# A round of two steps with three blocks of pairs, four single banks for the maxima, and twelve steps ahead

## The chip, the core and the metric

One core of a Trainium2 chip. The metric is device time in microseconds (us), the median of several executions; durations come from one execution under the hardware profiler. TensorE (PE) multiplies, VectorE (DVE) and ScalarE (ACT) read its results out of PSUM (eight banks of 512 float32 columns on 128 partitions), GpSimd (POOL) works in SBUF, SyncE (SP) and GpSimd issue transfers.

## What is computed

Input x is [4, 1024, 128]. Two layers, each with a residual:

```python
x = x + attn(layernorm(x))      # time mixing with a decaying scan (k, v, r), per batch
x = x + ffn(layernorm(x))       # below
# ffn: six nodes, each a multi-head attention over 1024 tokens, 8 heads of 16 columns
for c in range(6):
    nsrc = min(c + 1, 5); snode = c - nsrc
    q = ew[c, 0] * (nodes[c - 1] @ We[eq] + be[eq])
    k = ew[c, 1] * (nodes[snode] @ We[ek] + be[ek])
    v = ew[c, 2] * (nodes[snode + nsrc // 2] @ We[ev] + be[ev])
    nodes[c] = act_w[c] * mha(q, k, v, Wq[c], Wk[c], Wv[c], Wo[c]) + q
out = layernorm(nodes[5])
```

The softmax needs the maximum of each query's scores over all keys, since the scores are large here.

## The kernel before

**Units, groups, steps.** One attention (a node c of a batch b) is a unit; there are 24, in the order BATCH_OF. A unit has 4 groups (4 heads of one half of the queries: HG = 4, NHALF = 2), a group has 8 steps (NCH = 8 chunks of 128 keys). So a unit has UC = 32 steps and the whole has STEPS = 768. One step makes four score tiles (`scores`, L526: a chunk's 128 keys by 512 queries of one head, in one of three PSUM banks "ring"), ScalarE turns each into exponentials (L853, into `e_ring` with ten slots), and the value product (`weighted`, L571, L588: four heads side by side in the array, 512 query columns, float32) adds them up in the context bank over the group's eight steps.

**Maxima.** LOOKAHEAD = 14 steps ahead of the scores of a group, its scores are multiplied a first time the other way round (`maxima` of TensorE, L545, L566: 128 queries by 512 keys, two products a tile for the 1024 keys) into one of two double banks (`wide`, `WIDE_BANKS`), and VectorE reduces the 1024 columns to one maximum (`maxima` of VectorE, L1127, L1133). A group has 16 tiles, two to a step. When a group is finished (`finished`, L292, at s + LOOKAHEAD = 0 modulo 8), VectorE splits the maxima in two parts and transposes them (`split_high`, `split_low`, `turn_squares`: L1138, L1142, L1151), SP stores the rows and loads them one step later into two extra rows of `q_aug` (`store_rows`, `load_rows`: L1403, L1415), so that the second score product subtracts the maximum by itself.

**TensorE's order** is written out by hand (L660 to L695). A step is two halves. In each half: score, maxima, score, maxima, where a score and the maxima product behind it use different rows of the array and start together (a pair); then a half (256 columns) of the value product of the step before. In a step that has an extra product (`product_of`: the k, q and v products of the next units, the output products of the one before, final transposes; `KH_AT`, `OUT_AT`, `TURN_AT`, `V_AT`, `QH_AT`), that product stands in place of the first half's value product, in a ring bank, and the value product is done whole in the second half. A maxima tile waits until VectorE has reduced the tile two before (`v_mx`, L555).

**Before step 0** there is a stage of LOOKAHEAD steps with maxima only, with fillers (L426) and the time mixing of the first batches between (`mix`, at the places of MIX_AT); the mixing of the last parts (i = 6, 7) is spread over units 1 to 5. From ALONE = STEPS - LOOKAHEAD on there are no maxima any more, scores go round five banks. The last group has a way of its own at the end (`project_last`, `last_group`, `last_norm`).

**Other engines.** ScalarE evicts the extra products between the second and third exponential of a step (`stages`, L791) and the context after each group (L868). VectorE evicts v (`evict_v`, L998) and takes the reciprocal of the denominators at step 3 of a unit, second half (L1074). POOL splits k and q in two parts (L1233, L1235) and moves them (L312). SP stores and spreads the reciprocals at step 4 (`spread_rden`, L1443, L1450).

Of the kernel before, what the change touches and what calls it, by code (L numbers as in the profile page):

```python
# [18 lines left out]
LOOKAHEAD = 14  # L19
E_SLOTS = 10  # L20
Q_SLOTS = (0, 1, 0)
# [12 lines left out]
def build(nc, x, time_decay, mix_k, mix_v, mix_r, Wk, Wv, Wr, Wo, ln_g, ln_b, ew, act_w, We, be,  # L34
# [25 lines left out]
    with ctx:  # L60
# [46 lines left out]
        max_neg = sb("max_neg", [P, 2, NR])  # L107
# [28 lines left out]
        wide = [ctx.enter_context(nc.psum_tensor(f"wide{i}", [P, S], F32)) for i in range(2)]  # L136
        context = ctx.enter_context(nc.psum_tensor("context", [P, BANK], F32))
        bank = ([t[:, :] for t in ring] + [t[:, k * BANK:(k + 1) * BANK] for t in wide for k in range(2)] + [context[:, :]])
        WIDE_BANKS, CTX_BANK = ((3, 4), (5, 6)), 7
# [86 lines left out]
        KH_AT, OUT_AT, TURN_AT, V_AT, QH_AT = (5, 9), (13, 17), (18, 19), (21, 25), (30, UC + 1)  # L226
# [7 lines left out]
        FOLDS_AT, VALUES0_AT, ONES_AT = (-13, -12, -10, -8, -7), (-4, -3), 4  # L234
        BIAS0_AT, BIASES_AT = (29, -13), (0, 2)
# [5 lines left out]
        def turns_then_steps(turns, steps=()):  # L241
# [5 lines left out]
            turns_then_steps((7, 7, 8, 17, 17, 17, 17, 17, 18, 21, 24, 24, 28, 29, 30, 30, 31, 31, 32), (-14, -13, -12, -12, -9)),  # L247
            turns_then_steps((7, 8, 21, 23, 26, 26, 26, 26, 28, 29, 29, 29, 32),
# [15 lines left out]
        def final_steps(u):  # L264

            if u + 1 < LAST:
                return (19, 22), (20, 23), (21, 24), 26, 30
            return (19, 21), (20, 22), (21, 23), 24, 28
# [4 lines left out]
        def q_steps(u):  # L273

            if u in (1, 2):
                first = UC * (u - 1)
                return (first + 2, first + 3), first + 5
            first = UC * (u - 2)
            return (first + QH_AT[0], first + QH_AT[1]), first + UC + 3
# [21 lines left out]
        where = {}  # L301

# [42 lines left out]
        def tensor_program(e):  # L345
# [9 lines left out]
            def next_bank():  # L355
                ring_turn[0] += 1
                if alone[0]:
                    return ALONE_BANKS[ring_turn[0] % len(ALONE_BANKS)]
                return (ring_turn[0] - 1) % 3

# [138 lines left out]
            def project_last(at):  # L499

                c, b = CELLS[LAST]
                where["out", LAST, 1] = at
                bk = free_bank(at)
                e.matmul(bk[:, :], w_edge_q[:, c, :], node_ring[:, b, c % 2, half_of(1)], start=True, stop=False)
                e.wait_ge(v_ctx, 1)
                e.matmul(bk[:, :], w_o[0:HG * DH, c, :], ctxT[0:HG * DH, half_of(1)], start=False, stop=False)
                e.wait_ge(a_cv, GROUPS)
                e.wait_ge(g_to_values, 1)
                e.wait_ge(v_mx, GROUPS * TILES)
                e.matmul(bank[WIDE_BANKS[0][0]][:, :], to_values[:, :], last_raw, start=True, stop=True).then_inc(p_last_den, 1)  # L510
                for _ in range(LAST_FILLERS):
                    e.matmul(bank[WIDE_BANKS[1][0]][:, :], w_time_t[:, 0, :], w_time_t[:, 0:CPB, :], start=True, stop=True)
                e.wait_ge(d_w_last, DMA * HG)
                e.wait_ge(v_ctx, 3)
                e.matmul(bk[:, :], w_last[:, :], last_raw, start=False, stop=True).then_inc(p_o, 1)
                freed[at] = (a_oa, 2 * LAST + 2)

            def final_turn(u, hf, at):
                c, b = CELLS[u]
                where["turn", u, hf] = at  # L520
                e.wait_ge(a_oa, 2 * u + 2 if u < LAST else 2 * u + 1 + hf)
                node = node_ring[:, b, (c + 1) % 2, half_of(hf)]
                turn_four(at, halves_of(node), p_ft)
                freed[at] = (a_ft, 2 * b + hf + 1)

# [19 lines left out]
            def maxima(w, kh):  # L545
# [4 lines left out]
                h = hg * HG + hj  # L550
                first = (h % 2) * ROWS
                q0 = qh * BANK + qt * P
                if kh == 0:
                    if w >= 2:
                        e.wait_ge(v_mx, w - 1)  # L555
                    else:
                        for i in WIDE_BANKS[w]:
                            free_bank(i)
# [3 lines left out]
                if u == 0 and qh == 0 and t % (2 * CPB) == 0 and kh == 0:  # L562
                    pair = h // 2
                    e.wait_ge(d_q0[pair], DMA * Q_MOVES)
                    e.wait_ge(d_k0[pair], DMA * K_MOVES)
                done = e.matmul(wide[w % 2][:, half_of(kh)], q_aug[first:first + SPLIT, u % 2, h // 2, q0:q0 + P].bitcast(F32R),  # L566
                                k_aug[first:first + SPLIT, u % 2, h // 2, half_of(kh)].bitcast(F32R), start=True, stop=True)
                if kh == 1:
                    done.then_inc(p_mx, 1)
# [24 lines left out]
            def product_of(s):  # L594

                u, r = divmod(s, UC)
                nxt, prev = u + 1, u - 1
                if 1 <= nxt < UNITS:
                    if r in KH_AT:
                        return lambda: head_k(nxt, KH_AT.index(r), next_bank())  # L600
                    if r in V_AT:
                        return lambda: project_v(nxt, V_AT.index(r), next_bank())
                for unit in (nxt, nxt + 1):
                    if 1 <= unit < UNITS and s in q_steps(unit)[0]:
                        return lambda: head_q(unit, q_steps(unit)[0].index(s), next_bank())
                if 0 <= prev < LAST:
                    if r in OUT_AT:
                        return lambda: project_out(prev, OUT_AT.index(r), next_bank())
                    if CELLS[prev][0] == NODES - 1 and r in TURN_AT:
                        return lambda: final_turn(prev, TURN_AT.index(r), next_bank())  # L610
                for hf, (project_at, turn_at) in enumerate(LAST_AT):
                    if s == project_at:
                        return (lambda: project_last(next_bank())) if hf else (lambda: project_out(LAST, 0, next_bank()))
                    if s == turn_at:
                        return lambda: final_turn(LAST, hf, next_bank())
                return None


# [40 lines left out]

            for s in range(-LOOKAHEAD, LAST_STEP):  # L660
                product = product_of(s)
                z = s - 1
                if s == ALONE:
                    alone[0] = True
                    for w in range(2):
                        freed[WIDE_BANKS[w][1]] = (v_mx, GROUPS * TILES - 1 + w)
                if ALONE <= s < STEPS:
                    for k in range(HG):
                        scores(s, k)
                    if product:  # L670
                        product()
                    weighted(z, slice(0, BANK), True, True)
                    continue
                for half in range(2):
                    w = 2 * (s + LOOKAHEAD) + half
                    for k in range(2):
                        if 0 <= s < STEPS:
                            scores(s, 2 * half + k)
                        if w < GROUPS * TILES:
                            maxima(w, k)  # L680
                    if s < 0:
                        keep_busy(CTX_BANK, BANK // 2)
# [965 lines left out]
```

## Time and profile before

| | us |
|---|---|
| runs of the kernel before | 2264.27, 2265.6 (median), 2288.34 |
| the profiled execution, its own time | 2265.8 |
| its span, first to last instruction | 2264.0 |
| mean granted TensorE clock | 0.998 of full speed |

A busy time is the sum of an engine's instructions; for TensorE their ends are modelled, so what counts there is the distance from start to start. A row of the timeline merges instructions of one kind ("x4") from the start of the first to the end of the last.

### The profile page before, as it was taken

To read this page: it belongs to the slowest core of one execution; us is meant where nothing else is said; L and a number is where in the kernel's file an instruction comes from. 1 tells how busy PE (TensorE), PEld (TensorE's weight loads), DVE (VectorE), ACT (ScalarE), POOL (GpSimd) and SP (SyncE) were. 2 spreads that over 40 slices of the span, in tenths; PEclk is the share of its full clock that TensorE was granted. 3 is DMA by queue.
4 is the path that set the end of the run, shared out by engine and by line. 5 is a ranking of instruction groups with operands and counts; after the bars stand their busy time and mean duration, and the time that the engine had idled before them with its cause. 6 is when DMAs were issued, how large, how long until landed. Compare 5 with 4: busy or idle time off the path is not lost.

```text
span 2264.0 us, 46280 instructions
## 1 busy us (share of the span) xinstructions
PE 2231.4 (99%) x17991; PEld 848.7 (37%) x17991; DVE 2055.1 (91%) x2254; ACT 1829.0 (81%) x3431; POOL 529.3 (23%) x667
## 2 busy tenths in 40 slices
PE   7999999999999999999999999999999999999997
PEld 3533333333333333333333333333333333333332
DVE  6989999999999999999998999999999999989995
ACT  4277888888888888888888888888888888888886
POOL 4431230221312202202112112122022022321313
PEclk9999999999999999999999999999999999999999
DMA  4230332422313314224223233133132242241301
GB/s 126 64 72 25 81 71 49 89 64 66 80 46 91 71 33 92 60 61 85 64 57 81 55 69 80 36 78 80 34 82 62 49 85 54 61 95 42 74 25 53
DMA packets 87546, 149.55 MB, mean 66 GB/s; under 512 B 35147, under 2 KB 49951, under 8 KB 87327
## 3 DMA queue, kind: packets, MB, share of 16 engines
q0 software_dynamic: 28224, 94.13, 19.2%
q1 hardware_dynamic: 59102, 52.46, 9.2%
q8 instruction: 142, 2.33, 0.4%
q14 instruction: 78, 0.63, 0.1%
HBM read 42.36 MB, written 14.91 MB: 25 GB/s over the span
## 4 chain that ended last, share of the span: by engine, by line
PE 95%; DVE 2%; issue 1%; ACT 1%; SPq 0%; POOL 0%; DMA 0%; POOLq 0%; ACTq 0%; DVEq 0%
PE ring L540 43%; PE context L588 36%; PE ring L482 2%; PE ring L471 2%; PE ring L463 2%; PE ring L491 2%; PE ring L496 2%; PE wide L566 2%; DVE max_neg L1133 1%; PE context L426 1%; PE ring L369 0%; ACT e_ring L853 0%; PE ring L394 0%; PE ring L391 0%; PE ring L405 0%
## 5 line engine op out<-in xcount | busy, mean ns | idle before, releaser
L1133 DVE TENSOR_REDUCE max_neg<-wide 128x1 f32<-128x1024 f32 x1536 | 1850.4, 1220 | 142.2 <-PE wide L566 136.4
L853 ACT ACTIVATE e_ring<-ring 128x512 f32<-128x512 f32 x3052 | 1658.2, 597 | 286.6 <-PE ring L540 147.6
L566 PE MATMUL wide<-k_aug,q_aug 48*128 48x512 f32 x3072 | 1121.3, 444 | 2.3 <-DVE max_neg L1133 1.4
L540 PE MATMUL ring<-q_aug,k_aug 50*128 50x512 f32 x3052 | 1114.1, 444 | 0.0
L588 PE MATMUL context<-e_ring,v_aug 128*32 128x256 f32 (+1 forms) x10664 | 938.4, 424 | 1.8 <-ACT raw L868 1.6
L540 PEld LDWEIGHTS ring<-q_aug,k_aug 50*128 50x128 f32 x3052 | 455.7, 184 | 749.7 <-ACT e_ring L853 550.3
L566 PEld LDWEIGHTS wide<-k_aug,q_aug 48*128 48x128 f32 x3072 | 457.9, 184 | 12.9 <-issue 6.5
L588 PEld LDWEIGHTS context<-e_ring,v_aug 128*32 128x32 f32 x10664 | 209.9, 107 | 477.0 <-issue 340.9
L342 POOL DMA_DIRECT2D src<-node_dram x40 | 22.9, 572 | 633.2 <-PE ring L482 633.2
L1233 POOL CAST q_part<-q_part 128x512 fp32r<-128x512 f32 x46 | 28.1, 611 | 476.7 <-ACT q_part L778 302.0
L312 POOL DMA_DIRECT2D q_aug<-q_part x138 | 72.1, 522 | 126.3 <-PE ring L540 126.3
L1190 POOL TENSOR_TENSOR rstd<-vareps,neg_half 128x4 f32<-128x4 f32 x24 | 26.9, 1122 | 219.6 <-DVE vareps L897 219.4
L1259 POOL TENSOR_TENSOR ctxT<-ctxT,rden_bc 128x1024 f32<-128x1024 f32 x23 | 54.7, 2377 | 92.3 <-DMA rden_bc<-rden_dram 92.3
L312 POOL DMA_DIRECT2D k_aug<-k_part x138 | 70.0, 514 | 15.1 <-PE ring L540 9.8
L745 ACT ACTIVATE node_ring<-ring,col 128x512 f32<-128x512 f32 x47 | 32.3, 688 | 48.7 <-PE ring L496 40.8
L1235 POOL TENSOR_TENSOR k_part<-k_part 128x512 f32<-128x512 f32 x47 | 60.3, 1283 | 4.9 <-DVE src L902 1.2
L1235 POOL TENSOR_TENSOR q_part<-q_part 128x512 f32<-128x512 f32 x47 | 60.2, 1281 | 4.0 <-POOL k_part L1235 0.2
L868 ACT ACTIVATE raw<-context 128x512 f32<-128x512 f32 x96 | 58.0, 604 | 0.8 <-PE context L588 0.8
L471 PE MATMUL ring<-node_ring,w_q 128*128 128x512 f32 x92 | 51.8, 645 | 0.1
L491 PE MATMUL ring<-node_ring,w_edge_q 128*128 128x512 f32 x92 | 51.8, 644 | 0.0
L1233 POOL CAST k_part<-k_part 128x512 fp32r<-128x512 f32 x46 | 28.3, 615 | 82.9 <-ACT k_part L764 47.5
L496 PE MATMUL ring<-ctxT,w_o 128*128 128x512 f32 x92 | 47.0, 592 | 0.0
(241 smaller groups left out, 890.8 us busy)
## 6 DMA issues: line engine op xcount, KB each, us to landing
q_aug<-q_part POOLq DMA_DIRECT2D x138, 256.0 KB, 4.5
k_aug<-k_part POOLq DMA_DIRECT2D x138, 256.0 KB, 7.1
src<-node_dram POOLq DMA_DIRECT2D x40, 512.0 KB, 7.2
ctxT<-raw SPq DMA_DIRECT2D x380, 32.0 KB, 2.0
rden_bc<-rden_dram SPq DMA_DIRECT2D x23, 512.0 KB
node_dram<-node_ring SPq DMA_DIRECT2D x16, 512.0 KB, 2.9
q_aug<-rows_dram SPq DMA_DIRECT2D x192, 8.0 KB
node_ring<-in_L_attn_x SPq DMA_DIRECT2D x4, 512.0 KB, 4.9
```

The costliest lines, as they stand in the source:

```text
L312: e.dma_start(aug[first + slot:first + SPLIT:len(slots), u % 2, :, :], part[parity:P:2, slots[slot], :]).then_inc(signal, DMA)
L471: e.matmul(bk[:, :], w_q[:, c, :], node_ring[:, b, c % 2, half_of(hf)], start=True, stop=True).then_inc(p_qh, 1)
L491: e.matmul(bk[:, :], w_edge_q[:, c, :], node_ring[:, b, c % 2, half_of(hf)], start=True, stop=False)
L496: e.matmul(bk[:, :], w_o[:, c, :], ctxT[:, half_of(hf)], start=False, stop=True).then_inc(p_o, 1)
L540: e.matmul(bk[:, :], k_aug[first:first + AUG, u % 2, h // 2, chunk * P:(chunk + 1) * P].bitcast(F32R), q_aug[first:first + AUG, u % 2, h / ...
L566: done = e.matmul(wide[w % 2][:, half_of(kh)], q_aug[first:first + SPLIT, u % 2, h // 2, q0:q0 + P].bitcast(F32R), k_aug[first:first + SPL ...
L588: done = e.matmul(bank[CTX_BANK][j * VW:(j + 1) * VW, columns], v_aug[:, u % 2, chunk, hg * HG + j, :], e_ring[:, (HG * z + order_of(z).in ...
L853: e.activation(e_ring[:, n % E_SLOTS, :], bank[where["st", n]][:, :], ACT.Exp, scale=EXP_SCALE).then_inc(a_exp, 1)
L868: e.activation(raw[:, G % 2, :], bank[CTX_BANK][:, :], ACT.Copy).then_inc(a_cv, 1)
L1133: e.tensor_reduce(max_neg[:, G % 2, row:row + 1], wide[w % 2][:, :], AX_X, ALU.max, negate=True).then_inc(v_mx, 1)
L1233: step(e.tensor_copy(high.bitcast(F32R), x))
L1235: signal(e.tensor_tensor(x, x, high, ALU.subtract), signal_to)
```

## The change

LOOKAHEAD is 12. Two steps form a round. TensorE's order in it:

```diff
-            for s in range(-LOOKAHEAD, LAST_STEP):
-                product = product_of(s)
...
+            for s in range(0, ALONE, 2):
+                pair(s, 0)
+                pair(s, 1)
+                if s > 0:
+                    weighted(s - 2, second_half, False, True)
+                pair(s, 2)
+                pair(s, 3)
+                pair(s + 1, 0)
+                if s > 0:
+                    weighted(s - 1, whole, True, True)
+                mix_at(s)
+                pair(s + 1, 1)
+                pair(s + 1, 2)
+                pair(s + 1, 3)
+                for kind, unit, hf in products(s + 1):
+                    product(kind, unit, hf)
+                weighted(s, first_half, True, False)
+                mix_at(s + 1)
```

The maxima products go round four single banks (the same PSUM as the two double ones), and the extra products take a bank of that round too, no longer one of the ring. A maxima product waits until VectorE has freed its own bank, written four products before. A tile whose two banks are not neighbours in memory, and every even tile from 88 on, is reduced in two halves, each of which frees its bank; the others are one instruction over both banks:

```diff
-        KH_AT, OUT_AT, TURN_AT, V_AT, QH_AT = (5, 9), (13, 17), (18, 19), (21, 25), (30, UC + 1)
+        K_AT, OUT_AT, TURN_AT, V_AT, Q_AT = (5, 9), (13, 17), 19, (21, 25), (29, UC + 1)
...
+        def in_halves(w):
+
+            return w >= SPLIT_FROM and w % 2 == 0 or MAX_BANK_OF[2 * w] > MAX_BANK_OF[2 * w + 1]
...
-                e.wait_ge(p_mx, w + 1)
-                e.tensor_reduce(max_neg[:, G % 2, row:row + 1], wide[w % 2][:, :], AX_X, ALU.max, negate=True).then_inc(v_mx, 1)
+                if in_halves(w):
+                    for kh, b in enumerate((first, second)):
+                        e.wait_ge(p_mx, 2 * w + kh + 1)
+                        e.tensor_reduce(max_neg[:, G % 2, kh, row:row + 1], wide[:, b, :], AX_X, ALU.max, negate=True).then_inc(v_mx, 1)
+                else:
+                    e.wait_ge(p_mx, 2 * w + 2)
+                    e.tensor_reduce(max_neg[:, G % 2, :, row], wide[:, first:second + 1, :], AX_X, ALU.max, negate=True
+                                    ).then_inc(v_mx, 1)
...
             def split_high(G):
-                step(e.tensor_tensor(max_part[:, G % 2, :, 0, :].bitcast(F32R), both, both, ALU.max))
+                e.tensor_tensor(max_all[:, G % 2, :, :], one, two, ALU.min)
+                step(e.tensor_tensor(max_part[:, G % 2, :, 0, :].bitcast(F32R), one, two, ALU.min))
```

So each tile leaves two values, and the group's end joins them with one operation more. ScalarE evicts an extra product behind the last exponential of the round, and the context behind the fifth; an exponential waits for a freed slot of `e_ring` once a step, not twice:

```diff
+            for s in range(0, ALONE, 2):
+                for k in range(HG):
+                    exponential(s, k)
+                exponential(s + 1, 0)
+                if s > 0 and s % NCH == 0:
+                    evict_context(s // NCH - 1)
+                mix_at(s)
+                for k in range(1, HG):
+                    exponential(s + 1, k)
+                for kind, unit, hf in products(s + 1):
+                    evict(kind, unit, hf)
+                mix_at(s + 1)
```

VectorE evicts v in the second half of its step; SP's `spread_rden` is cut in two (`store_rden` at step 4, `spread_rden` at step 5); the final steps of a batch come one step later; the mixing that stood at steps -14 and -13 stands at -12. At the very end the last half of the last output is made in two parts of 256 columns: two output banks, the reciprocal and its product twice with 256 columns each, and the last matmul, the eviction and the transposes in two parts.

## Rows read from the trace of the kernel before

**Rows 1.** The page's first part: busy time, share and instructions of each engine.
```profile
PE 2231.4 (99%) x17991; PEld 848.7 (37%) x17991; DVE 2055.1 (91%) x2254; ACT 1829.0 (81%) x3431; POOL 529.3 (23%) x667
```

**Rows 2.** The page's fourth part: the chain that ended last, by engine.
```profile
PE 95%; DVE 2%; issue 1%; ACT 1%; SPq 0%; POOL 0%; DMA 0%; POOLq 0%; ACTq 0%; DVEq 0%
```

**Rows 3.** Timeline of PE in plain steps: start us, us, engine, line, operation, out<-in.
```profile
1014.85 0.49 PE L540 MATMUL ring<-q_aug,k_aug 50*128 50x512 f32 x1
...
1015.18 0.39 PE L540 MATMUL ring<-q_aug,k_aug 50*128 50x512 f32 x1
...
1015.51 0.64 PE L588 MATMUL context<-e_ring,v_aug 128*32 128x256 f32 x8
1016.08 0.49 PE L540 MATMUL ring<-q_aug,k_aug 50*128 50x512 f32 x1
```

**Rows 4.** Timeline of PE in a step with a q product.
```profile
1010.91 1.12 PE L471 MATMUL ring<-node_ring,w_q 128*128 128x512 f32 x2
...
1012.62 1.07 PE L588 MATMUL context<-e_ring,v_aug 128*32 128x512 f32 x8
1013.62 0.49 PE L540 MATMUL ring<-q_aug,k_aug 50*128 50x512 f32 x1
```

**Rows 5.** Timeline of PE at an output product.
```profile
2208.59 1.13 PE L491 MATMUL ring<-node_ring,w_edge_q 128*128 128x512 f32 x2
...
2210.51 0.50 PE L540 MATMUL ring<-q_aug,k_aug 50*128 50x512 f32 x1
```

**Rows 6.** Windows, L1133 alone: window, its length, busy time (count), clock, DMA share, GB/s.
```profile
736.00:1906.00 1170.00, 1027.10 (x852) 1.00 0.29 64
```

**Rows 7.** Timeline of DVE around a group's end and a reciprocal.
```profile
1021.07 1.22 DVE L1133 TENSOR_REDUCE max_neg<-wide 128x1 f32<-128x1024 f32 x1 [0.51 <-PE wide L566]
1022.33 0.17 DVE L1138 TENSOR_TENSOR max_part<-max_neg 128x16 fp32r<-128x16 f32 x1
...
1022.95 4.70 DVE L1133 TENSOR_REDUCE max_neg<-wide 128x1 f32<-128x1024 f32 x4
...
1028.02 1.16 DVE L1133 TENSOR_REDUCE max_neg<-wide 128x1 f32<-128x1024 f32 x1
```

**Rows 8.** Timeline of PE and DVE: data to reduction, and reduction to freed bank.
```profile
1001.60 10.67 DVE L1133 TENSOR_REDUCE max_neg<-wide 128x1 f32<-128x1024 f32 x9 [0.24 <-issue]
...
1002.71 0.50 PE L540 MATMUL ring<-q_aug,k_aug 50*128 50x512 f32 x1
1002.88 0.49 PE L566 MATMUL wide<-k_aug,q_aug 48*128 48x512 f32 x1
...
1013.96 0.39 PE L566 MATMUL wide<-k_aug,q_aug 48*128 48x512 f32 x1
...
1014.42 1.23 DVE L1133 TENSOR_REDUCE max_neg<-wide 128x1 f32<-128x1024 f32 x1 [0.43 <-PE wide L566]
```

**Rows 9.** Timeline of ACT: an exponential after idling, three in a row near the end.
```profile
1014.21 0.60 ACT L853 ACTIVATE e_ring<-ring 128x512 f32<-128x512 f32 x1 [0.48 <-PE ring L540]
...
2220.62 1.57 ACT L853 ACTIVATE e_ring<-ring 128x512 f32<-128x512 f32 x3
```

**Rows 10.** Timeline of DVE: the eviction of v, 512 columns, and the reduction behind it.
```profile
1077.02 0.68 DVE L998 TENSOR_TENSOR v_aug<-ring,v_bias 128x512 f32<-128x512 f32 x1
1077.63 1.23 DVE L1133 TENSOR_REDUCE max_neg<-wide 128x1 f32<-128x1024 f32 x1
```

**Rows 11.** Windows of all engines: window, length, PE, PEld, DVE, ACT, POOL busy (count), clock, DMA.
```profile
59.00:107.00 48.00, 47.73 (x220) 29.71 (x220) 46.07 (x79) 11.43 (x45) 18.79 (x20) 1.00 0.18 55
107.00:210.00 103.00, 101.38 (x768) 39.65 (x764) 94.37 (x117) 75.18 (x140) 31.59 (x39) 1.00 0.24 51
```

**Rows 12.** Timeline of SP: the maxima's rows stored and loaded.
```profile
1023.06 0.59 SPq L1403 DMA_DIRECT2D rows_dram<-max_turn  x1
1025.05 1.32 SPq L1415 DMA_DIRECT2D q_aug<-rows_dram  x2
```

**Rows 13.** Timeline of DVE in the last group: the reciprocal of its denominators.
```profile
2248.46 3.36 DVE L1024 RECIPROCAL mixing<-wide 128x512 f32<-128x512 f32 x1 [2.28 <-PE wide L510]
```

More of the change, by code:

```diff
@@ L276, in q_steps, with products @@
                 first = UC * (u - 1)
[L277 removed]
+                return (first + 3, first + 3), first + 5
             first = UC * (u - 2)
[L279 removed]
+            return (first + Q_AT[0], first + Q_AT[1]), first + UC + 3
+        def products(s):
+            u, r = divmod(s, UC)
+            nxt, prev = u + 1, u - 1
+            found = []
+            if 1 <= nxt < UNITS:
+                found += [("k", nxt, hf) for hf in range(2) if r == K_AT[hf]]
+                found += [("v", nxt, hf) for hf in range(2) if r == V_AT[hf]]
+            for unit in (nxt, nxt + 1):
+                if 1 <= unit < UNITS:
+                    found += [("q", unit, hf) for hf in range(2) if s == q_steps(unit)[0][hf]]
+            if 0 <= prev < LAST:
+                found += [("out", prev, hf) for hf in range(2) if r == OUT_AT[hf]]
+                if CELLS[prev][0] == NODES - 1 and r == TURN_AT:
+                    found += [("turn", prev, hf) for hf in range(2)]
+            return found
         def max_tile(t):
@@ L524, in final_turn, with last_turn @@
                 freed[at] = (a_ft, 2 * b + hf + 1)
+            def last_turn(ats):
+                c, b = CELLS[LAST]
+                node = halves_of(node_ring[:, b, (c + 1) % 2, half_of(1)])
+                for part, at in enumerate(ats):
+                    where["last turn", part] = at
+                    e.wait_ge(a_oa, 2 * LAST + 2 + part)
+                    bk = free_bank(at)
+                    for j in range(CPB // 2):
+                        done = e.transpose(bk[:, j * P:(j + 1) * P], node[CPB // 2 * part + j], ident[:, :])
+                    done.then_inc(p_ft, 1)
             def scores(s, k):
@@ L592, in weighted, with pair, product, mix_at @@
                     done.then_inc(p_ctx, 1)
[L594 to L616, printed above, removed]
+            def pair(s, k):
+                scores(s, k)
+                h = HG * (s + LOOKAHEAD) + k
+                if h < 2 * GROUPS * TILES:
+                    maxima(h)
+            def product(kind, unit, hf):
+                make = {"k": head_k, "q": head_q, "v": project_v, "out": project_out, "turn": final_turn}[kind]
+                make(unit, hf, next_max_bank())
+            def mix_at(s):
+                for i, k in mix_stages(s):
+                    mix(i, k, next_bank)
             e.wait_ge(g_ident, 1)
@@ L746, in evict_out, with evict_last @@
                              bias=col[:, C_BQ + c:C_BQ + c + 1]).then_inc(a_oa, 1)
+            def evict_last():
+                c, b = CELLS[LAST]
+                for part in range(2):
+                    e.wait_ge(p_o, 2 * LAST + 2 + part)
+                    e.activation(node_ring[:, b, (c + 1) % 2, half_of(1)][:, half_of_bank(part)],
+                                 bank[where["last", part]][:, half_of_bank(0)], ACT.Identity,
+                                 bias=col[:, C_BQ + c:C_BQ + c + 1]).then_inc(a_oa, 1)
             def order_heads():
```

289 lines of the change are left out of this document (159 added, 130 removed), and 2 rows, old and new, of the table MIX_AT.

## The prediction

> **What bounds the kernel now.** I read the engine shares first: TensorE is busy 99% of the span, VectorE 91%, ScalarE 81% [rows 1], and the chain that ended last is 95% TensorE [rows 2]. So the order and size of TensorE's instructions set the time, and VectorE is the engine that could take over. The timeline of plain steps shows how TensorE's time is made up [rows 3]. A half step is two pairs (a score product and a maxima product that start together, in different rows of the array) and half of a value product. Pair to pair takes 0.33 us (1014.85 to 1015.18), the second pair to the value product 0.33, the value product 0.57 (1015.51 to 1016.08), together 1.23. In a step with an extra product the value product is whole and takes 1.00 (1012.62 to 1013.62); from the extra product's start to the value product it is 1.71, less two pairs 1.05 to 1.06 for the extra product [rows 4]. An output product takes 1.92 [rows 5]. A unit of 32 steps is then 24 x 2.46 + 6 x (1.32 + 1.06 + 1.00) + 2 x (1.32 + 1.92 + 1.00) = 87.8 us; 852 reductions, two to a step, in 1170 us give 87.9 [rows 6]. The sum closes, so TensorE hardly waits.
>
> VectorE's side: four reductions in a row take 4.70 us, the last of them 1.22, so they start 1.16 apart when data is there. The work at a group's end (two small operations and a transpose) puts 1.88 between two starts (1021.07 to 1022.95), so it costs 0.72 beside a reduction. The fourth of the four starts at 1026.43 and, with a reciprocal between, the next one at 1028.02: 1.59, so the reciprocal costs 0.43 [rows 7]. A reduction starts 0.46 after the start of its last matmul (1013.96 to 1014.42), and a bank is written 0.06 after its end: the reduction from 1001.60 ends at 2.82 and the held maxima matmul starts at 1002.88, 0.17 after its partner, and all behind it is 0.17 later [rows 8]. Such waits I put at 0.15 a unit, since the sum above leaves no more, and since a group mostly ends right behind a product step, where VectorE has idle time (it sat idle 0.51 before 1021.07).
>
> **Part 1, the round of two steps.** Four blocks of pairs and four half value products (4.92 us) become blocks of 2, 3, 3 pairs with half, whole, half: 8 x 0.33 + 2 x 0.57 + 1.00 = 4.78, so 0.14 less for each merged pair of halves. A product step had a whole product already. Of 32 steps 24 had halves, so 48 halves and 8 wholes become 32 and 16: 8 x 0.14 = 1.12 us gained a unit. That a third pair costs 0.33 like the others isn't shown anywhere; the one spacing between pairs is the nearest row. Extra products cost what they did.
>
> ScalarE doesn't come into the way. Its exponentials last 0.60 and start 0.48 apart when data is there (three in 1.57), and start 0.59 after the score's start (1013.62 to 1014.21) [rows 4, 9]; eight to a round are 3.8 of 4.78. Following the three score banks through a round, the bank of the sixth score is asked for 0.8 us after it is free, the tightest is the first pair of the next round, 0.3 after.
>
> **Part 2, single banks and halves.** Bank n is written again four maxima matmuls later. By the code, 908 of 1536 tiles are reduced in halves: all even ones from tile 88 on (724), the rest where the two banks aren't neighbours. No row has a reduction of one bank. The addition of 512 columns out of a bank lasts 0.68 and the next reduction starts 0.61 after it [rows 10]; half of a 1.16 start distance is 0.58, the duration without overlap 0.68. I take 0.61 between starts and 0.68 for its length, ends 0.55 and 0.68. VectorE's round is then 2 x 1.16 + 4 x 0.61 = 4.76, against 4.64 before: no slack left against 4.78, where it had 0.28 against 4.92. The halves add 908 x 0.06 = 54 us of VectorE time, which by itself sets nothing. (The Trainium skill, "Vector Engine (DVE) Microarchitecture Reference", section 5.2 Measured stream behaviour on trn2, speaks against splitting: every instruction pays some 75 ns beside 1.04 ns a column, so an estimate by that page is 0.61 for a half and 1.14 for a whole; by it rival B's short half falls away. The trace has 1.16 for a whole, 2% more, and no half.)
>
> The group's end gains one small operation, so 0.72 becomes 0.82 (ends 0.73 and 0.90: nothing, or the 0.17 of the like one at 1022.33 [rows 7]). And it moves. With twelve steps ahead it falls at the start of the round of steps 4 and 5 modulo 8. Extra products stand at the ends of the rounds 0 and 4, so a full round without one lies before it. I follow one such pair of rounds, us from the first one's start. Maxima matmuls start at 0, 0.33, 1.23, 1.56, 1.90, 3.23, 3.56, 3.90. Reductions: halves at 0.47 and 1.08, whole at 2.03 (waits for its data), halves at 3.19 and 3.80, whole at 4.41. Then the group's end, so the next half starts at 4.41 + 1.16 + 0.82 = 6.39 and ends at 7.07. Its bank is wanted by the fifth matmul of the second round at 4.78 + 1.90 = 6.68 and comes at 7.12: TensorE waits 0.44. The half and whole behind it end at 8.84, and the seventh matmul waits 0.09 more. The product at the end of that round lets VectorE catch up, and the rounds 6 and 0 have no such wait. So 0.53 a group.
>
> Once a unit the reciprocal stands right before the group's end (step 3, second half, then step 4). It was hidden before (TensorE kept 1.23 there). Of its 0.43 some 0.05 falls together with the wait for the last reduction: 0.38 more. A unit: 4 x 0.53 + 0.38 = 2.50 us of waits, against 0.15 before, less 1.12: +1.23. Over the 22.6 units from step 32 to 756 that is **+28 us**.
>
> **Part 3, places that differ.** In unit 0 the even tiles are still whole, and a whole one holds the fifth matmul already in a fresh round (0.80 + 1.22 + 0.05 = 2.07 against 1.90). But VectorE was busy 94.4 of 103 us there, with mixing work on TensorE between [rows 11], so waits were there before: 0 to +5, I take +1.5. From step 36 on some 34 mixing operations of 0.7 to 1.2 us stand on VectorE, many now in rounds with a group's end. If each held TensorE for 0.3 us it were +10, at best it is 0; near the product steps most fit, so I take +2. The later k, q and value evictions and splits move by half a step; their next users are steps away: 0.
>
> **Part 4, twelve steps ahead.** The stage before step 0 has 24 tiles instead of 28. VectorE is busy 46.07 of 48 us in it [rows 11], so four reductions less are −4.7 (ends −5.2 and 0, the latter if the chains of mixing set it). Two steps more run with maxima (87.9 / 32 each, 5.5) and two fewer without, where ScalarE's four exponentials 0.48 apart and the switches make some 2.0 a step, −4.1: +1.4. The rows of maxima must be in q_aug four steps after the group's end, not six. Store and load are 2.0 us apart, the load's two issues last 1.32 [rows 12], and I give its landing 2 us, my estimate from the same 2.0 between a store and the load that waits for it: 5.3 us of 9.4 or more. Covered by 4 us; SP's store of reciprocals now lies between the two, 1.8 us, still covered.
>
> **Part 5, the end.** The last group's chain goes in halves, but its longest part, the reciprocal of 3.36 us [rows 13], is only cut, not shortened. Two reciprocals and two products in turn are some 0.2 longer. Behind them the last matmul, eviction, transposes and statistics each have half of the columns left: by half of 1.06, 0.68, 0.6 and 0.9 less their fixed parts 1.5 shorter. Two more matmul starts ahead cost 0.3: −1.0 (ends −2 and 0).
>
> **Sum.** 28 + 1.5 + 2 − 4.7 + 1.4 − 1.0 = +27 on the profiled execution's 2265.8, which stands 0.2 above the median: **2293 us**.
>
> **The rivals.** (B) The single-bank reduction is short (0.55 between starts, 0.60 long) and the group's end 0.73. Then the fifth matmul waits 0.23, the seventh 0.05, a unit 4 x 0.28 + 0.38 = 1.5, less 1.27: +0.2, times 22.6 is +5, the rest −1: 2270. For it: half of 1.16 is 0.58. Against it: every row of 512 columns here lasts 0.68. (C) Faster: no wait at all in the steady rounds. It decides where the path from the eighth matmul through whole reduction, group's end and first half (0.47 + 1.16 + 0.82 + 0.68 + 0.05 = 3.18) fits into the 2.79 between that matmul and the fifth of the next round. At 0.32 us of wait a group the change breaks even; with none a unit is 1.27 shorter, −29, the rest −4: 2233. For it: TensorE kept its pace through the ends of groups before. Against it: those came right behind a product. (D) Reductions of a bank don't overlap (0.68 between starts) and the group's end takes 0.90. VectorE's round is 5.04 and the waits 0.90 a group: (4 x 0.90 + 0.38 − 1.27) x 22.6 = +61: 2326. (E) The maxima's rows come late with four steps: each us beyond the margin of 4 costs 1 us in 94 groups; nothing in the trace takes so long.
>
> **How the numbers follow.** My forecast has 0.52 (own range 2278 to 2312), B 0.25, C 0.17, D 0.05, E 0.01. About what a measurement can tell from no change is 1%, 2243 to 2288. Of the forecast's 0.52, 0.12 lies under 2288. Slower by over 1%: 0.40 + 0.06 = 0.46. Within: 0.12 + 0.25 + 0.01 = 0.38. Faster: 0.16. The range reaches from 2243, which leaves C out, to 2316.
>
> **What would show it.** Half value products at 0.57 and wholes at 1.00, pairs 0.33 apart in blocks of three; half reductions of 0.68, starting 0.61 apart; in each group one maxima matmul, the fifth of the round of steps 4 and 5, held for 0.4 to 0.5 us by VectorE, longer once a unit; step 0 some 5 us earlier. The forecast is wrong if VectorE's releases cost TensorE less than 0.32 us a group, or if ScalarE or a DMA holds the scores.

## The result and the profile after

| | us |
|---|---|
| changed kernel, median of 4 runs (range) | 2386.1 (2376.8 to 2391.18) |
| kernel before, on the same chip | 2265.9 |
| ratio, 95% interval | 1.0502 (1.0428 to 1.0576): slower |
| forecast, range | 2293, 2243 to 2316 |
| profiled execution: its time, span, mean clock | 2382.87, 2381.0, 0.971 |

Slower was the likeliest sign, but the time lies 70 us above the top of the range. The first and fourth part of the page after, and two lines of its list of TensorE's waits (engine, line, what it waited for: us in total, times, longest us):

```profile
PE 2247.4 (94%) x16493; PEld 905.9 (38%) x16493; DVE 2069.2 (87%) x3260; ACT 1795.6 (75%) x3432; POOL 529.2 (22%) x667
...
PE 69%; DVE 17%; DMA 10%; issue 2%; SPq 1%; ACT 1%; POOL 0%; DVEq 0%; POOLq 0%; ACTq 0%
```

```profile
PE ring L601 <- DMA q_aug<-rows_dram: 56.3, 19, 4.3
PE wide L625 <- DVE max_neg L1231: 33.1, 87, 2.4
```

TensorE was busy 99% and is 94% [rows 1]; DMA was 0% of the chain and is 10% [rows 2]. The forecast had given a late transfer one chance in a hundred. TensorE waits 19 times for the maxima's rows, once in most units, and the chain around one such place shows what they waited for (start us, us, what):

```profile
1190.30 0.22 DVE max_turn L1253
1190.52 0.02 issue
1190.54 11.30 DMA rows_dram<-max_turn
1201.84 0.02 issue
1201.85 0.61 SPq L1519
1202.47 0.05 issue
1202.52 2.04 DMA q_aug<-rows_dram
1204.56 0.14 issue
1204.69 0.47 PE ring L601
```

The store of 16 KB took 11.3 us, where stores of the same rows mostly take 2.0 (as in [rows 12]); the load behind it was quick. SP's timeline has this at step 12 of 22 of the 23 units that prepare a next one: 7.0 to 11.6 us from the store's issue to the load's. GpSimd's timeline has a candidate just ahead of it: the six moves of the next unit's k ("k moves" below) and the load of a source. The lines are from the kernel after (GpSimd), then from the kernel before (SP, then GpSimd, at the same group's end):

```profile
1188.02 3.04 POOL L351 DMA_DIRECT2D k_aug<-k_part  x6 [0.56 <-PE ring L601]
1191.05 0.57 POOL L381 DMA_DIRECT2D src<-node_dram  x1
```

```profile
1045.79 0.54 SPq L1403 DMA_DIRECT2D rows_dram<-max_turn  x1
1047.74 1.29 SPq L1415 DMA_DIRECT2D q_aug<-rows_dram  x2
...
1048.35 3.04 POOL L312 DMA_DIRECT2D k_aug<-k_part  x6 [0.56 <-issue]
1051.38 0.57 POOL L342 DMA_DIRECT2D src<-node_dram  x1
```

Before, the rows of a unit's third group left 2.6 us ahead of the k moves; now they leave 2.5 us behind the moves' start. The DMA section of the page gives a k move as 256 KB and 7.1 us to landing. And what follows the wait is slow as well (windows: window, its length, busy PE, PEld, DVE, ACT, POOL, granted clock, DMA share, GB/s):

```profile
1190.00:1204.00 14.00, 10.43 (x72) 3.97 (x72) 9.87 (x14) 8.39 (x16) 1.62 (x4) 1.00 0.80 138
1204.70:1206.40 1.70, 1.70 (x14) 0.52 (x14) 1.17 (x2) 1.08 (x2) 0.00 (x0) 0.68 0.00 0
1206.40:1207.90 1.50, 1.50 (x10) 0.79 (x6) 0.36 (x2) 0.65 (x2) 0.00 (x0) 0.50 0.05 11
1207.90:1209.30 1.40, 1.40 (x10) 0.20 (x8) 1.40 (x2) 0.93 (x2) 0.00 (x0) 0.70 0.00 0
1209.30:1212.70 3.40, 3.40 (x24) 1.33 (x20) 2.00 (x3) 2.53 (x5) 0.00 (x0) 1.00 0.00 0
```

Until the store was done the sixteen DMA engines were 80% busy. TensorE, idle for 4.0 us, comes back and runs for 4.6 us at a granted clock of 0.68, 0.50 and 0.70 of full speed: 0.50 is the lower of its two levels, 1.2 GHz, and the other two are means over stretches that hold both. So a late row costs the wait and an aftermath.

Elsewhere the round has the order that was forecast, and is shorter. A plain round (start us, us; kernel after):

```profile
1152.94 0.64 PE L646 MATMUL context<-e_ring,v_aug 128*32 128x256 f32 x8
1153.51 0.49 PE L601 MATMUL ring<-q_aug,k_aug 50*128 50x512 f32 x1
...
1153.84 0.39 PE L601 MATMUL ring<-q_aug,k_aug 50*128 50x512 f32 x1
...
1154.09 0.39 PE L601 MATMUL ring<-q_aug,k_aug 50*128 50x512 f32 x1
1154.40 1.06 PE L646 MATMUL context<-e_ring,v_aug 128*32 128x512 f32 x8
1155.40 0.50 PE L601 MATMUL ring<-q_aug,k_aug 50*128 50x512 f32 x1
...
1157.52 0.64 PE L646 MATMUL context<-e_ring,v_aug 128*32 128x256 f32 x8
```

The half value product takes 0.57 and the whole 1.00, as in [rows 3, 4]. The second pair of a block starts 0.33 after the first, the third only 0.25 after the second, and the value product 0.31 behind that. From half to half the round takes 4.58 (4.59 in most), where I had 4.78.

### The profile page after: what moved, and what is told of

Its sections match the earlier page's. It is cut to its first block, busy times and chain, and to the rows that moved or that the text cites. A ratio compares the mean times of both kernels' runs of the same rounds, so it can differ in the third digit from the quotient of the medians.

```text
span 2381.0 us, 43523 instructions
## 1 busy us (share of the span) xinstructions
PE 2247.4 (94%) x16493; PEld 905.9 (38%) x16493; DVE 2069.2 (87%) x3260; ACT 1795.6 (75%) x3432; POOL 529.2 (22%) x667
## 4 chain that ended last, share of the span: by engine, by line
PE 69%; DVE 17%; DMA 10%; issue 2%; SPq 1%; ACT 1%; POOL 0%; DVEq 0%; POOLq 0%; ACTq 0%
PE context L646 26%; PE ring L601 24%; DMA rows_dram<-max_turn 8%; PE wide L625 8%; DVE max_neg L1234 8%; DVE max_neg L1231 6%; PE wide L527 2%; PE wide L516 2%; PE wide L508 2%; DMA q_aug<-rows_dram 2%; PE wide L536 1%; PE wide L541 1%; PE context L471 1%; DVE max_all L1240 1%; DVE max_part L1245 1%
## 5 line engine op out<-in xcount | busy, mean ns | idle before, releaser
L877 ACT ACTIVATE e_ring<-ring 128x512 f32<-128x512 f32 x3054 | 1603.2, 600 | 421.6 <-PE ring L601 419.7
L1231 DVE TENSOR_REDUCE max_neg<-wide 128x1 f32<-128x512 f32 x1816 | 1145.2, 682 | 184.6 <-PE wide L625 183.6
L625 PE MATMUL wide<-k_aug,q_aug 48*128 48x512 f32 x3072 | 1089.1, 448 | 42.0 <-DVE max_neg L1231 33.1
L601 PE MATMUL ring<-q_aug,k_aug 50*128 50x512 f32 x3054 | 1048.5, 441 | 57.8 <-DMA q_aug<-rows_dram 56.3
L1234 DVE TENSOR_REDUCE max_neg<-wide 128x2 f32<-128x1024 f32 x628 | 762.3, 1218 | 59.4 <-PE wide L625 58.5
L601 PEld LDWEIGHTS ring<-q_aug,k_aug 50*128 50x128 f32 x3054 | 501.7, 189 | 773.4 <-ACT e_ring L877 593.9
L625 PEld LDWEIGHTS wide<-k_aug,q_aug 48*128 48x128 f32 x3072 | 508.7, 188 | 95.8 <-DVE max_neg L1231 64.1
L886 ACT ACTIVATE raw<-context 128x512 f32<-128x512 f32 x96 | 57.7, 601 | 22.9 <-PE context L646 22.6
L805 ACT ACTIVATE node_ring<-wide,col 128x512 f32<-128x512 f32 x47 | 32.4, 689 | 39.8 <-PE wide L541 39.7
L516 PE MATMUL wide<-node_ring,w_q 128*128 128x512 f32 x96 | 54.2, 650 | 0.6 <-DVE max_neg L1234 0.6
L536 PE MATMUL wide<-node_ring,w_edge_q 128*128 128x512 f32 x94 | 53.9, 656 | 0.0
```

The costliest lines, as they stand in the source:

```text
L516: e.matmul(bk[:, :], w_q[:, c, :], node_ring[:, b, c % 2, half_of(hf)], start=True, stop=True).then_inc(p_qh, 1)
L601: e.matmul(bk[:, :], k_aug[first:first + AUG, u % 2, h // 2, chunk * P:(chunk + 1) * P].bitcast(F32R), q_aug[first:first + AUG, u % 2, h / ...
L625: e.matmul(bk[:, :], q_aug[first:first + SPLIT, u % 2, head // 2, q0:q0 + P].bitcast(F32R), k_aug[first:first + SPLIT, u % 2, head // 2, h ...
L877: e.activation(e_ring[:, n % E_SLOTS, :], bank[where["st", n]][:, :], ACT.Exp, scale=EXP_SCALE).then_inc(a_exp, 1)
L886: e.activation(raw[:, G % 2, :], bank[CTX_BANK][:, :], ACT.Copy).then_inc(a_cv, 1)
L1231: e.tensor_reduce(max_neg[:, G % 2, kh, row:row + 1], wide[:, b, :], AX_X, ALU.max, negate=True).then_inc(v_mx, 1)
```

## The experiments

Theory R after this reading: the rows are late, because their store meets the k moves. Rivals: the source load; VectorE's waits for banks at the group's ends; twelve steps in themselves; the clock.

### Which transfer

```diff
-                    if r == 10:
+                    if r == 14:
                         e.wait_ge(p_st, HG * s)
...
-                    if r == 14:
+                    if r == 16:
                         load_source(e, nxt, 1)
-                if 1 <= nxt < UNITS and half == 0 and r == 11:
+                if 1 <= nxt < UNITS and half == 0 and r == 15:
```

> Edit: in the changed kernel, GpSimd issues the k moves of the next unit at steps 14 and 15 (before: 10 and 11) and the source load at 16 (before: 14). Nothing else. Theory R (the rows of maxima are late): the store of these rows at step 12 stands among six k moves of 256 KB and takes 8 to 11 us where it takes 2 elsewhere; TensorE sits idle 3 to 4 us before step 16 of nearly every unit and then runs at a lower granted clock. With the moves behind it the store takes 2 to 3 us, the idle time goes, and the kernel falls from 2386 to 2235 to 2265 us. Rival V (my forecast's reason: VectorE frees the banks too late): nothing changes for VectorE, 2370 to 2390.

Measured: 2286.67 us, ratio 1.0099 (1.0083 to 1.0114). Store to load is now mostly 2.0 to 2.9 us (about 3.8 where the store of reciprocals stands between), and no row is waited for. That returns 99 of the 120 us. The edit also moved the load of the source; that load alone, moved to 16 with the k moves left in place:

> Edit: in the changed kernel only the source load (512 KB) moves from step 14 to 16; the k moves stay at 10 and 11. Theory R with the k moves as the cause: the store of rows at step 12 still takes 8 to 11 us, 2375 to 2392 us. Rival S (the source load is what the store and load of rows collide with): the store falls to some 3 us and the kernel to below 2300.

Measured: 2384.78 us (one run), 19 waits for rows with 57.0 us. So it is the k moves, not the source load.

### The clock behind the wait

Three matmuls into a score bank that is written anyway, ahead of the wait at a unit's third group:

```diff
+                if chunk == 0 and k == 0 and g == 2:
+                    for _ in range(3):
+                        e.matmul(bk[:, :], w_time_t[:, 0, :], w_time_t[:, 0:CPB, :], start=True, stop=True)
```

> Edit: in the changed kernel TensorE runs three 512-column float32 matmuls (2.6 us, results overwritten) into the score's own bank ahead of its wait for the rows at step 16 of each unit. The rows come no sooner. Theory C (part of the loss is the clock: after the idle time TensorE runs at half clock for some 4 us, which costs 1.5 to 2 us more a unit): the clock stays up, 25 to 45 us less than 2386. If the clock is no part of it: the same 2386, or up to 15 us more where the wait was shorter than the fillers.

Measured: 2362.51 us, ratio 1.0425 (1.0408 to 1.0442), and a mean clock of 0.99 instead of 0.971. The rows come as late as before; in the list of waits 8.8 us are left of 56.3, since the fillers stand in the wait's place. So some 24 us of the loss, a fifth, was TensorE at the lower clock after it had idled. It is rather more: the fillers take 2.8 us where nothing is waited for too, and unit 9, the only one whose rows were in time, became 2.7 us longer by them (90.0 against 87.3).

### Twelve steps in the old order

The kernel before with LOOKAHEAD = 12 and the places before step 0 moved to fit, nothing else:

> Edit: the kernel before with LOOKAHEAD 12, and what stood at steps -14 and -13 at -12; everything else as before (four blocks, double banks, no halves). Theory R: the collision comes with twelve steps ahead alone, since the group's end then falls at step 12 right behind the k moves: slower by 80 to 130 us, 2345 to 2395, with idle time of TensorE before step 16 of a unit. Rival V: the rounds of the kernel before have slack for VectorE, so within 10 us of 2266.

Measured: 2518.58 us, ratio 1.1105 (1.1079 to 1.113), well outside what was expected, at a mean clock of 0.942. Its list of waits and SP's timeline at a unit's start:

```profile
PE ring L540 <- DMA q_aug<-rows_dram: 105.4, 35, 4.7
```

```profile
1108.86 0.60 SPq L1403 DMA_DIRECT2D rows_dram<-max_turn  x1
1109.50 1.28 SPq L1443 DMA_DIRECT2D rden_dram<-rden_pack  x2
1113.43 0.64 SPq L1450 DMA_DIRECT2D rden_bc<-rden_dram  x1
1114.12 1.31 SPq L1415 DMA_DIRECT2D q_aug<-rows_dram  x2
```

Two rows a unit are late here: the one behind the k moves, and the one at step 4, where SP stands in the wait of the old `spread_rden` with the load of the rows queued behind it (5.3 us from store to load). The change cuts `spread_rden` into `store_rden` and `spread_rden`, which takes this wait away; the forecast had not asked for the purpose of that cut. With both removed (the k moves later as above, the spread at step 5 behind the load):

> The kernel before (its order on TensorE, its two double banks) with twelve steps ahead, but with both things out of the way that held the maxima's rows: the k moves at steps 14 and 15 and the source load at 16, and the spread of the reciprocals apart from their store, behind the load of the rows. It tells what twelve steps cost the old order once no transfer is late. Theory (the place of the group's end costs): with twelve it falls on step 4 modulo 8, two steps behind the extra product of step 1, and VectorE is no longer caught up there, so maxima products wait for banks at each group's end: some 0.3 to 0.5 us a group, a unit 89 to 90 against 88.0, total 2285 to 2315. Rival (only transfers made twelve dear): no row waited for, units 87.9 to 88.3 and a total of 2258 to 2272. If it is above 2350, the old order has a third trouble with twelve.

Measured: 2297.55 us, ratio 1.0142 (1.0123 to 1.0161), no row waited for, units of 89.1 against 87.9. The theory holds: with every transfer in time, twelve steps still cost the old order some 32 us, because the group's end comes two steps behind an extra product instead of right behind it. From start to start, the half step behind a group's end is 0.24 us longer at three of a unit's group ends and 0.5 at the one with the reciprocal, 1.2 a unit; in plain units of the kernel before, most show none.

### Fourteen steps in the new round

```diff
-LOOKAHEAD = 12
+LOOKAHEAD = 14
```

(with the places before step 0 as in the kernel before, and the final transposes of a batch also made after ALONE).

> Edit: the changed kernel with LOOKAHEAD 14 and the mixing at -14 and -13 as in the kernel before; the final transposes of the last but one unit, which then fall behind ALONE, go round the five banks there. Theory R plus W (the rows are in time again, and the group's end falls at step 2 modulo 8, right behind the round with an extra product, so the waits of 0.25 and 0.53 us on VectorE that the k-moves-later kernel still has at each group's end go too): the store of rows takes 2 to 4 us everywhere, a unit without mixing takes 86.0 to 86.8 us, the whole 2255 to 2275. If only the rows matter and not where the group's end falls: a unit of 87.3, 2280 to 2292.

Measured: 2231.45 us, ratio 0.9842 (0.9827 to 0.9858): lower than was expected, and faster than the kernel before by over 1%. The k moves stand where the change left them; the store leaves ahead of them again (1042.63 against 1045.20 in its trace). A plain unit takes 85.3. The theory had the waits at the group's ends gone with it. Three of a unit's four are smaller but still there: the round is still some 0.6, 0.4 and 0.4 us longer than the same round without a wait, 1.4 a unit.

### The halves

Late k moves and all even tiles in halves from tile 0 on, instead of from 88 on:

```diff
-        SPLIT_FROM = 2 * (UC + LOOKAHEAD)
+        SPLIT_FROM = 0
```

> Edit: k moves later as in e1, and every even tile from the first on is reduced in halves (SPLIT_FROM 0, before 88). Theory H: unit 0 is 17 us longer than in the kernel before because its even tiles are whole and hold two of the four banks till both columns halves are done; with halves 8 to 17 us of that go, 2270 to 2280. Rival: unit 0 is longer because of what stands where in the mixing (an operation of mixing behind the group's end on VectorE), then within 4 us of e1's 2287.

Measured: 2276.64 us, ratio 1.0042 (1.0028 to 1.0056), 10 us less than with late k moves alone; unit 0 takes 103.1 instead of 114.5. No even tile in halves (tiles whose banks are not neighbours stay in halves in every run; whether one instruction could take them was not tried):

```diff
-        SPLIT_FROM = 2 * (UC + LOOKAHEAD)
+        SPLIT_FROM = 2 * GROUPS * TILES
```

> Edit: k moves later as in e1, and no tile in halves but those whose two banks aren't neighbours. Theory H: a whole even tile holds the bank of the fifth maxima product of the round; by the hand recurrence TensorE waits 0.2 us in a round after a product and 0.6 in the others, some 5 to 8 us a unit, 2390 to 2460. Rival: the halves only add VectorE time (54 us of it), then 2265 to 2290.

Measured: 2665.67 us, ratio 1.1762 (1.1736 to 1.1788), far more than expected. The same with fourteen steps:

> The changed kernel with fourteen steps ahead, and no even tile reduced in halves (only the tiles whose two banks are not neighbours, where one instruction is impossible). With twelve steps and late k moves the same edit made 2287 into 2666. Theory (the round itself needs the halves: the third block's products come back to a bank four products later, before a whole reduction of both banks has ended, in every round wherever the group's end falls): units stay far above 90, total 2400 to 2700. Rival (the halves were needed only at the group's ends, which with fourteen stand behind a product step): units 86 to 90, total 2240 to 2340.

Measured: 2525.99 us, ratio 1.1173 (1.1138 to 1.1208), a plain unit 98.2. Lines from one plain round, TensorE and then VectorE:

```profile
1103.74 0.50 PE L601 MATMUL ring<-q_aug,k_aug 50*128 50x512 f32 x1
1104.12 0.49 PE L625 MATMUL wide<-k_aug,q_aug 48*128 48x512 f32 x1
...
1105.92 0.39 PE L601 MATMUL ring<-q_aug,k_aug 50*128 50x512 f32 x1
1106.44 0.50 PE L625 MATMUL wide<-k_aug,q_aug 48*128 48x512 f32 x1
```

```profile
1102.84 1.23 DVE L1238 TENSOR_REDUCE max_neg<-wide 128x2 f32<-128x1024 f32 x1 [0.86 <-PE wide L625]
1103.98 1.28 DVE L1235 TENSOR_REDUCE max_neg<-wide 128x1 f32<-128x512 f32 x2
1105.17 1.22 DVE L1238 TENSOR_REDUCE max_neg<-wide 128x2 f32<-128x1024 f32 x1
```

The matmul at 1104.12, 0.38 behind the score that it should start with, waited for a whole reduction (1102.84 to 1104.07), the one at 1106.44, 0.52 behind its score, for the next whole one (1105.17 to 1106.39), and VectorE idled 0.86 before the first of the two, because a whole one can't begin until both its banks are filled. Each engine waits for the other; the round takes 5.60 (1101.27 to 1106.87, whole to whole) instead of 4.59. So the round needs the halves everywhere: those of the even tiles add 21 us to VectorE's busy time (2039.7 to 2060.7, from this kernel to the same one with them) and take 295 us off the time. Unit 0, where the change leaves even tiles whole, pays for it.

Last, fourteen steps and halves from tile 0 on together:

> Edit: e5 and SPLIT_FROM 0 together: fourteen steps ahead, all even tiles in halves. If the rows, the place of the group's end and unit 0's whole tiles are all that the change loses, this is faster than the kernel before: 2240 to 2262.

Measured: 2225.03 us, ratio 0.9843 (0.9798 to 0.9889); unit 0 takes 99.9 instead of 108.4. It has the lowest median, 41 us under the kernel before. That it is faster than fourteen steps alone is not shown: its four runs reach from 2218.96 to 2243.55, and the two intervals overlap.

Side by side, in us:

| | the old order | the new round | and all even tiles in halves |
|---|---|---|---|
| 14 steps ahead | 2265.6 | 2231.45 | 2225.03 |
| 12 ahead, rows in time | 2297.55 | 2286.67 | 2276.64 |
| 12 ahead, k moves in place | 2518.58 (and the old spread) | 2386.1 | |

The round is worth 34 us with fourteen steps and 11 with twelve. It is the lookahead of twelve that spends it, twice: 55 us in the new round (32 in the old order) where every row is in time, and 99 us more by the place of the k moves. Most of the 55 is VectorE's work at the group's end. The two kernels compared there also differ in where the k moves stand, but less their waits from start to start their plain units are alike (87.3 − 3.5 = 83.8 and 85.3 − 1.4 = 83.9), so in a plain unit these waits are the whole difference of 2.0.

## Why the prediction was wrong, point by point

Distances between the context evictions cut the span into stretches ("unit 0" reaches from its first eviction to that of unit 1; the profiled executions, of which the one with late k moves stands 6 above its median; changes against the kernel before, us):

| stretch | before | forecast | late k moves | after |
|---|---|---|---|---|
| to the first eviction | 139.9 | −4.7 | +4.8 | −1.7 |
| unit 0 | 97.2 | +1.5 | +17.3 | +16.8 |
| six units with mixing | 539.1 | +9.4 | +8.1 | +26.2 |
| to the last eviction | 1469.2 | +22 | −3.7 | +75.4 |
| end | 18.6 | −1.0 | +0.3 | +0.3 |
| sum | 2264.0 | +27 | +26.8 | +117.0 |

**The step that failed is part 4's landing of the rows**, "5.3 us of 9.4 or more. Covered by 4 us", and with it rival E's "nothing in the trace takes so long". The 2.0 us were read at one quiet place [rows 12] and taken for all four group ends of a unit. What GpSimd's queue issues at step 12 was not looked up, though the k moves were named in the code and their six issues stood in the trace. With 11.3 for the store, 0.6 for the issue and 2.0 for the landing the sum is 14, 4 to 5 us over the margin of 9.4, and the wait measured there was 4.0. Rival E's pricing, a us for a us in 94 groups, had the number of late groups too high (one a unit was late) and the price too low: of the 99 us at least some 24 were the clock behind the wait.

What makes the store slow is shown only as far as this: it is the k moves, since moving them and nothing else of weight returned the time, and it is those issued ahead of it. In 21 of the 22 late places of the kernel after, every k move issued ahead of the store had landed before the load could follow (in the other, one issued 0.2 us ahead of the store landed 0.2 late), while in five of them a k move issued behind it landed later. In unit 9, the one that escaped, a single k move stood ahead, issued 1.9 us before the store, and the store took 2.0 us. By the Trainium skill, "DMA: Bandwidth & Descriptors", section Queues, rings and completion order, a transfer's semaphore increment lands only after every earlier write of that DMA engine, across its queues. For the k moves the trace agrees with it (a small store done 13.8 us after the first of six 256 KB moves began). But in the old order with twelve steps five loads of a source, issued 1.7 to 3.3 us ahead of the store, landed 0.1 to 1.1 us after it was done. What each engine had written by then is not in the trace, so no run here tells that rule from plain sharing of the busy engines, and the reason stays open.

**Part 1** was right in kind, and too small. That a third pair costs 0.33 "isn't shown anywhere", it said; it costs 0.24 to 0.25. With two such pairs a round and 16 rounds, a unit is some 3 us shorter than worked out: 83.8 without waits, where the forecast's 87.8 − 1.12 is 86.7. Next to the rows, which it put at nothing, this is the largest mis-sized term, 2.9 x 22.6 = 66 us, and it hid behind the rest.

**Part 2** found the mechanism. Two halves take 1.28 together (0.60 apart, 0.68 long), and the group's end 0.80 beside a reduction where 0.82 was put. The kernel with late k moves, VectorE then TensorE:

```profile
1032.17 1.22 DVE L1234 TENSOR_REDUCE max_neg<-wide 128x2 f32<-128x1024 f32 x1
1033.42 0.17 DVE L1240 TENSOR_TENSOR max_all<-max_neg 128x16 f32<-128x16 f32 x1
...
1034.13 1.26 DVE L1231 TENSOR_REDUCE max_neg<-wide 128x1 f32<-128x512 f32 x2
```

```profile
1033.96 0.39 PE L601 MATMUL ring<-q_aug,k_aug 50*128 50x512 f32 x1
...
1034.20 0.39 PE L601 MATMUL ring<-q_aug,k_aug 50*128 50x512 f32 x1
1034.84 0.50 PE L625 MATMUL wide<-k_aug,q_aug 48*128 48x512 f32 x1 [0.25 <-DVE max_neg L1231]
1035.27 1.07 PE L646 MATMUL context<-e_ring,v_aug 128*32 128x512 f32 x8
```

It is the fifth maxima product of the round, as forecast. It starts 0.64 after its score, where 0 is the rule. The profile's bracket says 0.25, because TensorE is idle only from the score's end on: what a held matmul costs is read from start to start. From whole to whole the round takes 5.34 instead of 4.59, so 0.75 a group against 0.53 forecast, and 1.03 against 0.91 in the group with the reciprocal (a round of 5.62); with the extra product behind it, which comes 0.05 late as well, that is 3.5 a unit for 2.5. The faster round is the reason: VectorE's work stayed and TensorE returns sooner. The forecast's own recurrence, with the distances measured (0.33 and 0.24 between pairs, a round of 4.58, the group's end 0.80), has the bank free at 7.07 and wanted at 4.58 + 1.80 = 6.38, a wait of 0.69 where it had 0.44. Together with part 1 a plain unit is 87.3, where 89.1 was forecast and mostly 87.9 measured before.

One thing the forecast had no row for: the small operation at the group's end is at times far longer than its 0.17 us. VectorE, then GpSimd, in the kernel with fourteen steps:

```profile
1381.67 1.39 DVE L1244 TENSOR_TENSOR max_all<-max_neg 128x16 f32<-128x16 f32 x1
```

```profile
1380.64 2.38 POOL L1365 TENSOR_TENSOR ctxT<-ctxT,rden_bc 128x1024 f32<-128x1024 f32 x1 [4.47 <-DMA rden_bc<-rden_dram]
```

It ends 0.04 us after GpSimd's. The small operations of the group's end last over 0.35 us in 56 places of these twelve traces; in each of them one of GpSimd's tensor operations is running, and they end 0.03 to 0.04 us behind it. Reductions that lie wholly under such an operation keep their 0.68 (133 of them in the kernel after). It reaches TensorE: with fourteen steps the round behind that group's end takes 4.73 us where the operation lasts 0.37, 5.20 where it lasts 0.85 and 5.74 where it lasts 1.39. With twelve steps it happens where the final steps of a batch run on GpSimd (2.31 us in unit 20, and TensorE waits 2.4 there). No run moves GpSimd's operation away, so what that would save is not shown.

**Part 3** was off by 16 us in unit 0. That a whole tile "holds the fifth matmul already in a fresh round (2.07 against 1.90)" was written down and then priced at nothing to five; the kernel without halves shows 1.0 us in each round, and more where mixing operations stand before it. With late k moves TensorE waited there for up to 2.6 us on a whole reduction and ran at a clock of 0.66 and 0.74 in two stretches of 20 us, where it had 1.00 before. The six units with mixing gain nothing from the shorter round: late k moves leave them at +8.1, a plain unit's −0.6 six times and some 12 us of mixing, for which 2 had been taken.

**Part 4's other terms.** The stage before step 0 is worth what was said: the old order with twelve steps reaches its first eviction at 134.2, 5.8 us sooner, for −4.7 forecast. In the kernels of the new round it is not seen: their first eviction comes at 138.1 to 144.8, and what sets it there no run takes apart. **Part 5**: the end did not get 1.0 shorter, it got 0.3 longer in every kernel of the new round; why is not shown either.

That the kernel with late k moves comes out at 2286.67, 6 us from the forecast, is no success of the sum: by the table the units after the mixing are 26 us below their forecast, unit 0 is 16 above and the stretch ahead of it 10.

**The rivals.** B (2270) and C (2233) need waits that were smaller than forecast; they were larger. C's number is reached, at 2231, but by fourteen steps: then the group's end stands right behind an extra product and the list of TensorE's waits holds 9 us for the maxima products, where with twelve and late k moves it had 42 (start to start 1.4 us a unit against 3.5). D's two prices (0.68 apart, 0.90) were not there, though the wait of 0.8 a group is nearly the 0.90 that it had worked out from them. E was the case, with a chance of 0.01.

## What to carry to other kernels

When a lookahead is shortened, list every transfer that any queue has in flight in the new margin, for each of the places where the margin is used; a store of 16 KB was as late here as the k moves issued ahead of it. A round that is tight on two engines needs its periodic work behind the place where the bounding engine is given something extra to do, so the phase of the lookahead matters as much as its length. And a bank should be freed as soon as it is read: a reduction over two banks saved its own engine 21 us here and cost the kernel 295.

## What the runs showed of the hardware

- Of three pairs of concurrent matmuls in a row (50 and 48 rows, 512 columns) the second starts 0.33 us after the first and the third 0.24 after the second; with two pairs only, nothing shows the shorter distance.
- A 16 KB store to DRAM takes 2.0 us between store and dependent load in a quiet place, and 7.0 to 11.6 us where it is issued 1.9 to 6.4 us behind the start of six moves of 256 KB on GpSimd's queue. Behind one such move alone it took 2.0 us.
- After 4.0 us without a matmul TensorE ran at 1.2 GHz part of the time: a granted clock of 0.68, 0.50 and 0.70 over 4.6 us. Three matmuls put in the place of the wait took the mean clock of the run from 0.971 to 0.99.
- A VectorE operation on small tiles in SBUF (128x16, 0.17 us) that met a GpSimd tensor operation of 2.4 us ended 0.03 to 0.04 us after it, up to 2.34 us long; reductions out of PSUM beside it kept their length.
- Losses come larger than their waits: with twelve steps, late k moves and no even tile in halves, TensorE's list of waits sums to some 205 us in the five lines that wait for VectorE's maxima, and the time rose by 379, at a mean clock of 0.952 instead of 0.988.
